# Order of the convolution kernel's set-up, and of the head's first transposes, in a state-space and gated-MLP kernel

## The chip, the cores and the metric

One core of a Trainium2 chip runs the program. The metric is the device time of one execution in microseconds (us); three timed runs of the kernel before are at hand, and one profiled execution.

## The reference, cut to what matters

`x` is 2 x 1024 rows of 512. Each row is normalised. From the normalised rows come a convolution along the row, whose 512 taps are made from 64 complex states (Lambda, p, q, B, Ct), and a gated MLP whose three weights carry low-rank additions (rank 16).

```
xn = _layernorm(x)
# convolution kernel K (512 taps), from the states
g = 2.0 / step * ((1.0 - Omega) / (1.0 + Omega))
denom = g[:, None] - Lambda[None, :]
cauchy = lambda v: (v[None, :] / denom).sum(-1)
k00, k01, k10, k11 = cauchy of Ct*B, Ct*p, q*B, q*p
at_roots = c * (k00 - k01 * (1.0 / (1.0 + k11)) * k10)
K = ifft(at_roots, L).real
s = causal convolution of xn with K, plus D * xn
h1 = xn @ (w1 + 2 B1 A1).T ; h3 = xn @ (w3 + 2 B3 A3).T
g = silu((silu(h1) * h3) @ (w2 + 2 B2 A2).T)
out = x + s * g
```

## The kernel before

**Tiling.** The 2048 rows are cut into four blocks of 512 (block 0, a loop over blocks 1 and 2, block 3). The 1376 hidden units are cut into 11 tiles, j = 0 to 10. For each j there are three places: "gate" (product with w1's tile into `h1`), "up" (w3's tile into `h3`) and "down" (w2's tile j-1 into the four banks `f`). Every float32 operand is split in a high and a low part of type fp32r, and a product is three matmuls (lines 939 to 941), each 128x128 by 128x512. Five engines run instruction streams of their own, each in the order in which the code is written, and they meet by semaphores.

**Folds, in block 0 only.** `fold(kind, j)` on TensorE multiplies the low-rank factors of weight `kind` (1, 3 or 2) and tile j into one of two PSUM banks `spare0`, `spare1`, used in turn. VectorE adds it to the loaded weight (`fold_add`, line 728), which also frees the bank; ScalarE casts the high part (`fold_hi`, line 592); VectorE subtracts to get the low part (`fold_lo`, line 743; three of them are done by GpSimd). TensorE waits for both before it uses the tile (`wait_split`). A fold thus takes a bank that the fold two before it must have left. Folds (3, j+2) stand at place "up" and (1, j+2) at "gate" of tile j, (2, j) at "down". `hidden_mul` (line 792) multiplies silu(h1) by h3, ScalarE casts its high part (line 632), `hidden_lo` (line 797) gives the low part. The cast of tile j waits until TensorE has finished `down(j-1)` (semaphore `g_used`).

**The convolution kernel, beside the folds.** ScalarE scales a row of sines and cosines (line 671, waits for the load `trig_sb`). GpSimd turns that into denominators and their squared magnitude `mag`; then come three `fold_lo` of its own, then 35 small operations that make the vectors `vmat` ("the vectors"), then the product `res` with `1/mag`. VectorE makes the reciprocal in two halves at the places in `RECIPROCAL_AT`. TensorE multiplies `res` by `vmat` at `KAPPA_AT` into a spare bank ("kappa", line 1056); ScalarE copies it out (line 675); GpSimd works out the coefficients, stores them and loads them back as a row on all partitions (`coef_row`). VectorE multiplies the four parts of `dft_sb` by that row (`K_PRODUCTS_AT`) and sums them (`K_SUMS_AT`). The sum goes by three DMAs to the Toeplitz tile `tz`, which the convolution at the end of block 0 needs.

**The head.** TensorE runs the folds (1,0) and (3,0), transposes the four row tiles (`turn_rows(r)`), and the folds (1,1) and (3,1) stand between them. Per row tile ScalarE normalises (`rows_norm`), then casts the transposed tile (`rows_hi`), and VectorE makes its low part (`rows_lo`). The first 256 columns of tile 0 start when row tiles 0 and 1 are split. Beside that the factors of all other folds are split in `spread_hl` (lines 701, 887); after its low part SyncE issues six DMAs that lay them out in `lora_stack`, and behind these in the same queue the weights of the next tiles and `trig_sb`. `spare` and the table `SPARE` deal the banks in the order of use, so a moved kappa changes the banks of the folds between its old place and its new one.

Of the kernel before, what the change touches and what calls it, by code (L numbers as in the profile page):

```python
# [25 lines left out]
ALU = mybir.AluOpType  # L26
ACT = mybir.ActivationFunctionType
AXIS = mybir.AxisListType
# [151 lines left out]
RECIPROCAL_AT = [(2, "down"), (3, "down")]  # L180

KAPPA_AT = (5, "gate")
K_PRODUCTS_AT, K_SUMS_AT = (7, "gate"), (7, "up")
# [3 lines left out]
K_PARTS = D // P  # L187
# [59 lines left out]
def build(nc, x, xT, w1, w3, w2, lora, lora_st, lora_mv, s4_lanes, s4_vc, s4_bp, s4_scalars, trig, lanes, dft, outT):  # L247
    ctx = ExitStack()
    with ctx:
# [337 lines left out]
        def _(act):  # L587
# [6 lines left out]
            def rows_hi(r):  # L594
                act.wait_ge(xt_turned, r + 1)
                nc.scalar.copy(xt[:, 0, 0, :, r * P:(r + 1) * P],
                               f[r][:, :].rearrange("p (c u) -> p c u", c=DC)).then_inc(xhi_done, 1)
# [101 lines left out]
            rows_hi(0)  # L699
            act.wait_ge(spread_in, 32)  # L700
            nc.scalar.copy(spread_hl[:, 0, :], spread[:, :]).then_inc(spread_hi, 1)
            rows_norm(2)
            rows_hi(1)
# [14 lines left out]
        def _(dve):  # L718
# [108 lines left out]
            def body(b, par, par_next, first, last):  # L827
# [4 lines left out]
                for j in range(HT):  # L832
                    for place in ("gate", "up", "down"):
# [11 lines left out]
                        if first and (j, place) == K_PRODUCTS_AT:  # L845
                            dve.wait_ge(dft_in, 16)
                            dve.wait_ge(coef_row_in, 16)
                            for h in range(K_PARTS):
                                nc.vector.tensor_tensor(dft_sb[:, h, :], dft_sb[:, h, :], coef_row[:, :], ALU.mult) \  # L849
                                    .then_inc(k_products, 1)  # L850
                        if first and (j, place) == K_SUMS_AT:
                            dve.wait_ge(k_products, K_PARTS)
                            nc.vector.tensor_reduce(kcol[:, :], dft_sb[:, :, :], AXIS.X, ALU.add).then_inc(k_summed, 1)
                        if place == "up":
                            hidden_lo(b, j)
                        if first and (j, place) in RECIPROCAL_AT:
                            n = RECIPROCAL_AT.index((j, place))
                            dve.wait_ge(mag_ready, 1)
                            part = mag[:, n * D // len(RECIPROCAL_AT):(n + 1) * D // len(RECIPROCAL_AT)]
                            nc.vector.reciprocal(part, part).then_inc(inv_ready, 1)  # L860
                        for c in () if last else norm_at.get((j, place), ()):
                            next_shift(b + 1, c, par_next)
# [20 lines left out]
            fold_add(3, 0)  # L883
            fold_lo(1, 0)
            rows_lo(0)
# [3 lines left out]
            rows_lo(1)  # L889
# [15 lines left out]
        def _(pe):  # L905
# [66 lines left out]
            def start():  # L972
# [9 lines left out]
                turn_rows(0)  # L982
                fold(1, 1)
                turn_rows(1)
                fold(3, 1)
# [4 lines left out]
                for c in range(DC):  # L990
                    pe.matmul(h1[:, lo], w13_tile(1, 0, 0)[:, c, :], xt[:, 0, 0, c, lo], start=(c == 0), stop=False)
                turn_rows(3)
# [132 lines left out]
        def _(pool):  # L1125
            steps = [0]

            def then(ins):

                steps[0] += 1  # L1130
                ins.then_inc(s4_step, 1)
                pool.wait_ge(s4_step, steps[0])
# [59 lines left out]
            pool.wait_ge(den_ready, 3)  # L1192
            then(tt(den_im[:, :], den_im[:, :], res[:, :], ALU.add))
            then(tt(mag[:, :], den_re[:, :], den_re[:, :], ALU.mult))
            then(tt(res[:, :], den_im[:, :], den_im[:, :], ALU.mult))
            tt(mag[:, :], mag[:, :], res[:, :], ALU.add).then_inc(mag_ready, 1)
            for kind, j in POOL_LO:
                fold_lo(kind, j)

# [22 lines left out]
            pool.wait_ge(v_ready, 1)  # L1222

# [56 lines left out]
            pool.wait_ge(k_summed, 1)  # L1280
# [74 lines left out]
```

## Time and profile before

| | |
|---|---|
| median of 3 runs | 411.18 us (411.14 to 411.35) |
| the profiled execution | 411.04 us, of which its span is 409.2 us |
| TensorE matmuls busy | 403.8 us (99% of the span) |
| VectorE | 169.0 us (41%) |
| ScalarE | 106.6 us (26%) |
| GpSimd | 70.7 us (17%) |
| granted TensorE clock | 1.00 in the mean |
| chain that ended last | PE 93%, DVE 4%, issue 1% |

TensorE's busy time fills the span, so the time is the length of its stream plus the waits in it. The other engines count by what they make TensorE wait for. VectorE's 41% is a mean: in block 0 it is busy for 6 to 9 us of every 10, later for 2 to 4.

### The profile page before, as it was taken

The page shows a single profiled execution, that of the slowest core. Times are in us where ns is not written, and L with a number is a line of the kernel's source. Part 1 is how long each engine was busy: PE and PEld are TensorE (multiplying, and loading weights), DVE is VectorE, ACT ScalarE, POOL GpSimd, SP SyncE. Part 2 cuts the span into 40 slices and gives each one's busy share as a digit, 9 for nine tenths or more (in the row PEclk, how much of TensorE's full clock was granted, in tenths as well). Part 3 has the DMA queues.
Part 4 walks back from the last instruction along what each step waited for, and adds up shares of the span by engine and source line. Part 5 has one row for each costly group of instructions (what it writes and reads, how often), then busy time and mean ns, then how long its engine had stood idle before and what let it go on. Part 6 is the DMA issues. An engine that isn't in the chain of part 4 may idle for free.

```text
span 409.2 us, 5001 instructions
## 1 busy us (share of the span) xinstructions
PE 403.8 (99%) x1850; PEld 336.9 (82%) x1850; DVE 169.0 (41%) x264; ACT 106.6 (26%) x174; POOL 70.7 (17%) x140
## 2 busy tenths in 40 slices
PE   8999999999999999999999999999999999999996
PEld 8988888878888888888888888888888888888885
DVE  5777776783792322142343222133334111211125
ACT  7654332222351111222221111112222111111122
POOL 6237737510800114000000102300000000000000
PEclk9999999999999999999999999999999999999999
DMA  7673933403425101000016101000002000000002
GB/s 267 175 274 114 318 110 89 98 9 96 154 77 181 51 2 52 2 0 0 0 48 202 61 0 52 0 0 0 0 0 103 2 0 0 2 0 0 2 0 103
DMA packets 14514, 27.02 MB, mean 66 GB/s; under 512 B 2672, under 2 KB 4720, under 8 KB 14368
## 3 DMA queue, kind: packets, MB, share of 16 engines
q1 hardware_dynamic: 13872, 25.40, 19.3%
q0 software_dynamic: 336, 0.86, 1.1%
q10 hardware_dynamic: 288, 0.52, 0.3%
q8 instruction: 11, 0.18, 0.2%
q14 instruction: 7, 0.06, 0.0%
HBM read 21.48 MB, written 4.54 MB: 64 GB/s over the span
## 4 chain that ended last, share of the span: by engine, by line
PE 93%; DVE 4%; issue 1%; ACT 0%; DVEq 0%; POOL 0%; ACTq 0%; POOLq 0%
PE h L939 19%; PE h L940 19%; PE h L941 19%; PE f L939 10%; PE f L940 10%; PE f L941 10%; PE h L962 2%; PE spare L926 2%; PE h L970 1%; DVE raw L728 1%; PE spare L941 1%; PE spare L940 1%; PE spare L939 1%; PE spare L921 1%; DVE dft_sb L849 1%
## 5 line engine op out<-in xcount | busy, mean ns | idle before, releaser
L939 PE MATMUL h<-xt,w 128*128 (+2 forms) x340 | 131.2, 386 | 0.0
L940 PE MATMUL h<-xt,w 128*128 (+2 forms) x340 | 131.1, 386 | 0.0
L941 PE MATMUL h<-xt,w 128*128 (+2 forms) x340 | 131.1, 386 | 0.0
L941 PEld LDWEIGHTS h<-xt,w 128*128 128x128 f32 x340 | 63.9, 188 | 12.9
L939 PEld LDWEIGHTS h<-xt,w 128*128 128x128 f32 x340 | 63.9, 188 | 12.7
L940 PEld LDWEIGHTS h<-xt,w 128*128 128x128 f32 x340 | 63.9, 188 | 12.5
L792 DVE TENSOR_TENSOR g<-g,h 128x512 f32<-128x512 f32 x40 | 27.5, 688 | 108.5 <-PE h L941 108.3
L939 PE MATMUL f<-ghl,w2f 128*128 128x512 f32 x176 | 68.7, 390 | 0.8 <-DVE w2f L743 0.8
L797 DVE TENSOR_TENSOR ghl<-g,ghl 128x512 fp32r<-128x512 f32 x44 | 31.6, 718 | 90.2 <-ACT ghl L632 90.2
L940 PE MATMUL f<-ghl,w2f 128*128 128x512 f32 x176 | 68.6, 390 | 0.0
L941 PE MATMUL f<-ghl,w2f 128*128 128x512 f32 x176 | 68.5, 389 | 0.0
L632 ACT CAST ghl<-g 128x512 fp32r<-128x512 f32 x44 | 27.3, 621 | 156.4 <-PE f L941 143.5
L939 PEld LDWEIGHTS f<-ghl,w2f 128*128 128x128 f32 x176 | 33.0, 188 | 7.7 <-DVE w2f L743 1.0
L941 PEld LDWEIGHTS f<-ghl,w2f 128*128 128x128 f32 x176 | 33.0, 188 | 6.9
L940 PEld LDWEIGHTS f<-ghl,w2f 128*128 128x128 f32 x176 | 33.1, 188 | 6.5
L615 ACT ACTIVATE g<-h 128x512 f32<-128x512 f32 x40 | 23.9, 598 | 45.3 <-PE h L941 45.1
L728 DVE SCALAR_TENSOR_TENSOR raw<-spare,raw 128x512 f32<-128x512 f32 (+2 forms) x33 | 22.3, 677 | 2.2 <-DVE raw L728 1.1
L1138 POOL TENSOR_TENSOR scales<-moments,lane_c 128x2 f32<-128x2 f32 x6 | 1.6, 258 | 119.5 <-DVE moments L755 119.5
L592 ACT CAST w<-raw 128x512 fp32r<-128x512 f32 (+1 forms) x22 | 13.4, 610 | 29.8 <-DVE raw L728 29.7
L1138 POOL TENSOR_TENSOR normal_rows<-xres,scale_rows 128x512 f32 (+1 forms) x12 | 16.0, 1365 | 13.5 <-DMA scale_rows<-scales_scratch 13.5
L743 DVE TENSOR_TENSOR w<-raw,w 128x512 fp32r<-128x512 f32 (+1 forms) x17 | 12.7, 751 | 0.4 <-DVE raw L728 0.2
L592 ACT CAST w2f<-raw 128x512 fp32r<-128x512 f32 (+1 forms) x11 | 6.8, 622 | 18.1 <-DVE raw L728 18.1
(133 smaller groups left out, 309.9 us busy)
## 6 DMA issues: line engine op xcount, KB each, us to landing
raw<-w_dram SPq DMA_DIRECT2D x28, 256.0 KB, 4.1
xres<-xT_dram SPq DMA_DIRECT2D x4, 1024.0 KB, 7.0
outT_dram<-xres SPq DMA_DIRECT2D x15, 256.0 KB, 2.4
rows_next<-x_dram SPq DMA_DIRECT2D x4, 512.0 KB, 3.8
scale_rows<-scales_scratch SPq DMA_DIRECT2D x3, 512.0 KB, 4.0
dft_sb<-dft_dram SPq DMA_DIRECT2D x1, 1024.0 KB, 9.3
rows<-x_dram SPq DMA_DIRECT2D x2, 512.0 KB, 6.8
raw<-w_dram SPq DMA_DIRECT2D x4, 224.0 KB, 2.5
```

Of the source, the lines that this page charges most:

```text
L592: nc.scalar.copy(folded(kind, j, 0), raw_tile(kind, j)).then_inc(whi_done, 1)
L615: nc.scalar.activation(g[:, :], h1[:, :], ACT.Silu).then_inc(silu_done, 1)
L632: nc.scalar.copy(ghl[:, 0, :], g[:, :]).then_inc(ghi_done, 1)
L728: nc.vector.scalar_tensor_tensor(out=rt, in0=low, scalar=LORA_SCALE, in1=rt, op0=ALU.mult, op1=ALU.add) \
L743: nc.vector.tensor_tensor(folded(kind, j, 1), raw_tile(kind, j), folded(kind, j, 0).bitcast(F32), ALU.subtract).then_inc(wlo_done, 1)
L792: nc.vector.tensor_tensor(g[:, :], g[:, :], h3[:, :], ALU.mult).then_inc(g_done, 1)
L797: nc.vector.tensor_tensor(ghl[:, 1, :], g[:, :], ghl[:, 0, :].bitcast(F32), ALU.subtract).then_inc(glo_done, 1)
L926: mm = pe.matmul(bankt[:, n * units:(n + 1) * units], fac[:, a + c * P:a + (c + 1) * P], fac[:, bc + t0 * P:bc + t0 * P + units], start=Tr ...
L939: pe.matmul(out, w[1], m[0], start=start, stop=False)
L940: pe.matmul(out, w[0], m[1], start=False, stop=False)
L941: return pe.matmul(out, w[0], m[0], start=False, stop=stop)
L1138: return nc.gpsimd.tensor_tensor(out, a, c, op)
```

## The change

Four edits. (1) In the head TensorE turns row tile 1 ahead of fold (1,1), and fold (3,1) goes behind the first four matmuls of tile 0; ScalarE normalises row tile 2 and casts row tile 1 ahead of the spread factors' high half; VectorE takes row tiles 0 and 1 ahead of fold (1,0)'s low half and of the spread factors' low half. (2) GpSimd makes the vectors ahead of the denominators. (3) The second reciprocal moves from (3, "down") to (3, "up"), kappa from (5, "gate") to (4, "up"). (4) The products move from (7, "gate") to two at (6, "up") and two at (7, "gate"), the sum from (7, "up") to one half at (7, "gate") and one at (7, "up"); products, sums and reciprocal now stand ahead of `hidden_lo` of the same place.

```diff
-RECIPROCAL_AT = [(2, "down"), (3, "down")]
-KAPPA_AT = (5, "gate")
-K_PRODUCTS_AT, K_SUMS_AT = (7, "gate"), (7, "up")
+RECIPROCAL_AT = [(2, "down"), (3, "up")]
+KAPPA_AT = (4, "up")
+K_PRODUCTS_AT = {(6, "up"): (0, 1), (7, "gate"): (2, 3)}
+K_SUMS_AT = {(7, "gate"): slice(0, 2), (7, "up"): slice(2, 4)}
...
             rows_hi(0)
+            rows_norm(2)
+            rows_hi(1)
             act.wait_ge(spread_in, 32)
             nc.scalar.copy(spread_hl[:, 0, :], spread[:, :]).then_inc(spread_hi, 1)
-            rows_norm(2)
-            rows_hi(1)
...
-                        if first and (j, place) == K_PRODUCTS_AT:
+                        if first and (j, place) in K_SUMS_AT:
+                            parts = K_SUMS_AT[j, place]
+                            dve.wait_ge(k_products, parts.stop)
+                            nc.vector.tensor_reduce(kcol[:, parts], dft_sb[:, parts, :], AXIS.X, ALU.add).then_inc(k_summed, 1)
+                        if first and (j, place) in K_PRODUCTS_AT:
                             dve.wait_ge(dft_in, 16)
                             dve.wait_ge(coef_row_in, 16)
-                            for h in range(K_PARTS):
+                            for h in K_PRODUCTS_AT[j, place]:
...
-                        if place == "up":
-                            hidden_lo(b, j)
                         if first and (j, place) in RECIPROCAL_AT:
...
+                        if place == "up":
+                            hidden_lo(b, j)
...
+            rows_lo(0)
             fold_lo(1, 0)
-            rows_lo(0)
+            rows_lo(1)
             dve.wait_ge(spread_hi, 1)
             nc.vector.tensor_tensor(spread_hl[:, 1, :], spread[:, :], spread_hl[:, 0, :].bitcast(F32), ALU.subtract) \
                 .then_inc(spread_lo, 1)
-            rows_lo(1)
...
                 turn_rows(0)
+                turn_rows(1)
                 fold(1, 1)
-                turn_rows(1)
-                fold(3, 1)
                 turn_rows(2)
...
                     pe.matmul(h1[:, lo], w13_tile(1, 0, 0)[:, c, :], xt[:, 0, 0, c, lo], start=(c == 0), stop=False)
+                fold(3, 1)
                 turn_rows(3)
...
             pool.sem_inc(small_ready, 1)
-            pool.wait_ge(den_ready, 3)
...
-            for kind, j in POOL_LO:
-                fold_lo(kind, j)
...
             pool.wait_ge(v_ready, 1)
 
+            pool.wait_ge(den_ready, 3)
+            then(tt(den_im[:, :], den_im[:, :], res[:, :], ALU.add))
...
+            for kind, j in POOL_LO:
+                fold_lo(kind, j)
+
             pool.wait_ge(inv_ready, len(RECIPROCAL_AT))
...
-            pool.wait_ge(k_summed, 1)
+            pool.wait_ge(k_summed, len(K_SUMS_AT))
```

VectorE at tile 7, before: fold_add (1,9), the four products, `hidden_mul`, fold_lo (1,9), fold_add (3,9), the sum, `hidden_lo`.

```order
L728 SCALAR_TENSOR_TENSOR raw_76<-spare0,raw_76 128x448 [waits fold_ready,raw_in1]
L849 TENSOR_TENSOR dft_sb_86<-dft_sb_86,coef_row_77 128x512 [waits fold_added,coef_row_in,dft_in]
L849 TENSOR_TENSOR dft_sb_86<-dft_sb_86,coef_row_77 128x512 x3
L792 TENSOR_TENSOR g_57<-g_57,h3 128x512 [waits h3_ready,silu_done]
L743 TENSOR_TENSOR w13_49<-raw_76,w13_49 128x2x224 [waits whi_done]
L728 SCALAR_TENSOR_TENSOR raw_76<-spare1,raw_76 128x448 [waits fold_ready,raw_in5]
L853 TENSOR_REDUCE kcol_74<-dft_sb_86 128x4 [waits fold_added,k_products]
L797 TENSOR_TENSOR ghl_52<-g_57,ghl_52 128x512 [waits ghi_done]
```

VectorE from tile 6 "up" on, now: fold_add (3,8), two products, `hidden_lo(6)`, fold_lo (3,8), fold_add (2,6), the moments of rows 2 and 3, fold_lo (2,6).

```order
L729 SCALAR_TENSOR_TENSOR raw_76<-spare0,raw_76 128x512 [waits fold_ready,raw_in4]
L854 TENSOR_TENSOR dft_sb_86<-dft_sb_86,coef_row_77 128x512 [waits fold_added,coef_row_in,dft_in]
L854 TENSOR_TENSOR dft_sb_86<-dft_sb_86,coef_row_77 128x512
L798 TENSOR_TENSOR ghl_52<-g_57,ghl_52 128x512 [waits ghi_done]
L744 TENSOR_TENSOR w13_49<-raw_76,w13_49 128x512 [waits whi_done]
L729 SCALAR_TENSOR_TENSOR raw_76<-spare1,raw_76 128x512 [waits fold_ready,raw_in2]
L753 BN_STATS stats_61<-rows_1_94 128x6 [waits fold_added,rows_in1]
L756 BN_AGGR moments_62<-stats_61 128x2 [waits stats_done]
L753 BN_STATS stats_61<-rows_1_94 128x6 [waits rows_in1]
L756 BN_AGGR moments_62<-stats_61 128x2 [waits stats_done]
L744 TENSOR_TENSOR w2f_50<-raw_76,w2f_50 128x512 [waits whi_done]
```

The wait for `coef_row_in` stood behind fold_add (1,9); now it stands ahead of `hidden_lo(6)` and of all that follows it.

ScalarE at tiles 4 and 5, before: the high cast of the hidden tile 4, then the casts and the silu of the next places, and the copy of kappa.

```order
L632 CAST ghl_52<-g_57 128x512 [waits g_used,g_done]
L592 CAST w2f_50<-raw_76 128x512 [waits fold_added]
L615 ACTIVATE g_57<-h1 128x512 [waits glo_done,h1_ready]
L592 CAST w13_49<-raw_76 128x512 [waits fold_added]
L675 COPY kap_71<-spare0 128x32 [waits kappa_ready]
```

ScalarE there, now:

```order
L633 CAST ghl_52<-g_57 128x512 [waits g_used,g_done]
L676 COPY kap_71<-spare0 128x32 [waits kappa_ready]
L593 CAST w2f_50<-raw_76 128x512 [waits kappa_copied,fold_added]
L616 ACTIVATE g_57<-h1 128x512 [waits glo_done,h1_ready]
```

The copy of kappa moved up past two casts and a silu, and stands right behind the cast that waits for `g_used`.

VectorE in the head, before, from fold_add (3,0) on: the low half of fold (1,0), of row tile 0 (`f0`), of the spread factors, of row tile 1 (`f1`), of fold (3,0).

```order
L728 SCALAR_TENSOR_TENSOR raw_76<-spare1,raw_76 128x512 [waits fold_ready,raw_in4]
L743 TENSOR_TENSOR w13_49<-raw_76,w13_49 128x512 [waits fold_added,whi_done]
L765 TENSOR_TENSOR xt_51<-f0,xt_51 128x4x128 [waits xhi_done]
L887 TENSOR_TENSOR lora_spread_split_80<-lora_spread_79,lora_spread_split_80 128x708 [waits spread_hi]
L765 TENSOR_TENSOR xt_51<-f1,xt_51 128x4x128 [waits xhi_done]
L743 TENSOR_TENSOR w13_49<-raw_76,w13_49 128x512 [waits whi_done]
```

VectorE in the head, now:

```order
L729 SCALAR_TENSOR_TENSOR raw_76<-spare1,raw_76 128x512 [waits fold_ready,raw_in4]
L766 TENSOR_TENSOR xt_51<-f0,xt_51 128x4x128 [waits fold_added,xhi_done]
L744 TENSOR_TENSOR w13_49<-raw_76,w13_49 128x512 [waits whi_done]
L766 TENSOR_TENSOR xt_51<-f1,xt_51 128x4x128 [waits xhi_done]
L890 TENSOR_TENSOR lora_spread_split_80<-lora_spread_79,lora_spread_split_80 128x708 [waits spread_hi]
L744 TENSOR_TENSOR w13_49<-raw_76,w13_49 128x512 [waits whi_done]
```

The spread factors' low half, which SyncE's six stack loads wait for, moved one row down; those of the row tiles moved up.

## Rows read from the trace of the kernel before

**Rows 1.** Waits of TensorE's weight loads; us in total, times, longest.
```profile
PEld f L939 <- DVE w2f L743: 1.0, 1, 1.0
```

**Rows 2.** Timeline, TensorE, hidden tiles 7 and 8: start, length, instruction, idle before.
```profile
80.12 0.41 PE L939 MATMUL f<-ghl,w2f 128*128 128x512 f32 x1
...
88.78 0.45 PE L926 MATMUL spare<-lora_stack 128*128 128x224 f32 x2
...
90.07 0.50 PE L939 MATMUL f<-ghl,w2f 128*128 128x512 f32 x1 [0.84 <-DVE w2f L743]
```

**Rows 3.** Timeline, VectorE, hidden tiles 6 to 8.
```profile
72.48 0.69 DVE L728 SCALAR_TENSOR_TENSOR raw<-spare,raw 128x512 f32<-128x512 f32 x1
...
74.89 0.69 DVE L797 TENSOR_TENSOR ghl<-g,ghl 128x512 fp32r<-128x512 f32 x1 [1.72 <-ACT ghl L632]
...
78.80 0.66 DVE L743 TENSOR_TENSOR w2f<-raw,w2f 128x512 fp32r<-128x512 f32 x1
...
80.22 2.50 DVE L849 TENSOR_TENSOR dft_sb<-dft_sb,coef_row 128x512 f32<-128x512 f32 x4 [0.23 <-DMA coef_row<-coef_scratch]
...
84.55 2.29 DVE L853 TENSOR_REDUCE kcol<-dft_sb 128x4 f32<-128x2048 f32 x1 [0.16 <-DVE raw L728]
...
89.32 0.69 DVE L743 TENSOR_TENSOR w2f<-raw,w2f 128x512 fp32r<-128x512 f32 x1 [0.69 <-ACT w2f L592]
```

**Rows 4.** Timeline, TensorE and ScalarE around the kappa product.
```profile
52.48 0.40 PE L939 MATMUL f<-ghl,w2f 128*128 128x512 f32 x1
...
55.00 0.39 PE L941 MATMUL f<-ghl,w2f 128*128 128x512 f32 x1
...
58.41 0.95 PE L1056 MATMUL spare<-vmat,res 128*128 128x8 f32 x8
...
60.57 0.62 ACT L592 CAST w<-raw 128x512 fp32r<-128x512 f32 x1 [1.23 <-DVE raw L728]
...
61.10 0.18 ACT L675 COPY kap<-spare 128x32 f32<-128x32 f32 x1
```

**Rows 5.** Timeline of GpSimd on the convolution kernel.
```profile
40.38 0.69 POOL L1135 TENSOR_SCALAR vtmp<-lane_d,lane_c 128x1 f32<-128x1 f32 x2
...
54.02 1.62 POOL L1138 TENSOR_TENSOR res<-den_im,mag 64x512 f32<-64x512 f32 x1
...
71.78 0.97 POOL L1268 DMA_DIRECT2D coef_scratch<-coef  x1 [0.31 <-POOL coef L1138]
```

**Rows 6.** Waits of GpSimd and ScalarE on the denominators; us in total, times, longest.
```profile
POOL den_im L1138 <- ACT res L671: 13.2, 1, 13.2
...
ACT den_re L671 <- DMA trig_sb<-trig_dram: 1.2, 1, 1.2
```

**Rows 7.** DMA issues: tensors, queue, count, KB, median us from issue to landing.
```profile
coef_scratch<-coef POOLq DMA_DIRECT2D x1, 2.0 KB, 4.1
...
k_row<-kcol POOLq DMA_DIRECT2D x1, 2.0 KB, 1.7
```

**Rows 8.** Timeline, VectorE, hidden tile 3: the low half and a reciprocal.
```profile
47.20 0.71 DVE L797 TENSOR_TENSOR ghl<-g,ghl 128x512 fp32r<-128x512 f32 x1 [1.73 <-ACT ghl L632]
...
49.25 1.75 DVE L860 RECIPROCAL mag<-mag 128x256 f32<-128x256 f32 x1
```

**Rows 9.** Timeline, VectorE, head: the spread factors' low half.
```profile
11.60 0.89 DVE L887 TENSOR_TENSOR lora_spread_split<-lora_spread,lora_spread_split 128x708 fp32r<-128x708 f32 x1
```

**Rows 10.** Timeline, SyncE: the last of six stack loads.
```profile
16.77 0.60 SPq L545 DMA_DIRECT2D lora_stack<-lora_spread_split  x1
```

**Rows 11.** DMA issues of that stretch: KB, us from issue to landing.
```profile
lora_stack<-lora_spread_split SPq DMA_DIRECT2D x1, 204.0 KB, 3.9
```

**Rows 12.** Timeline, TensorE: the first fold that needs the stack.
```profile
21.33 0.40 PE L921 MATMUL spare<-lora_stack 128*128 128x512 f32 x1
```

**Rows 13.** Timeline, VectorE and TensorE: folds of tiles 3 and 4.
```profile
33.40 0.68 DVE L728 SCALAR_TENSOR_TENSOR raw<-spare,raw 128x512 f32<-128x512 f32 x1
...
34.14 0.64 PE L926 MATMUL spare<-lora_stack 128*128 128x256 f32 x4
```

More of the change, by code:

```diff
@@ L844, in body @@
                             late = now[-1:]
-                        if first and (j, place) == K_PRODUCTS_AT:
+                        if first and (j, place) in K_SUMS_AT:
[3 more added lines that the diff above has]
+                        if first and (j, place) in K_PRODUCTS_AT:
                             dve.wait_ge(dft_in, 16)
                             dve.wait_ge(coef_row_in, 16)
-                            for h in range(K_PARTS):
+                            for h in K_PRODUCTS_AT[j, place]:
                                 nc.vector.tensor_tensor(dft_sb[:, h, :], dft_sb[:, h, :], coef_row[:, :], ALU.mult) \
                                     .then_inc(k_products, 1)
-                        if first and (j, place) == K_SUMS_AT:
-                            dve.wait_ge(k_products, K_PARTS)
-                            nc.vector.tensor_reduce(kcol[:, :], dft_sb[:, :, :], AXIS.X, ALU.add).then_inc(k_summed, 1)
-                        if place == "up":
-                            hidden_lo(b, j)
                         if first and (j, place) in RECIPROCAL_AT:
@@ L1191, in _ @@
             pool.sem_inc(small_ready, 1)
-            pool.wait_ge(den_ready, 3)
[L1193 to L1196, printed above, removed]
-            for kind, j in POOL_LO:
-                fold_lo(kind, j)
             then(ts(vtmp[:, 0:1], lane_d[:, 3:4], lane_c[:, SIGN:SIGN + 1], ALU.mult))
@@ L1222, in _ @@
             pool.wait_ge(v_ready, 1)
+            pool.wait_ge(den_ready, 3)
+            then(tt(den_im[:, :], den_im[:, :], res[:, :], ALU.add))
+            then(tt(mag[:, :], den_re[:, :], den_re[:, :], ALU.mult))
+            then(tt(res[:, :], den_im[:, :], den_im[:, :], ALU.mult))
+            tt(mag[:, :], mag[:, :], res[:, :], ALU.add).then_inc(mag_ready, 1)
+            for kind, j in POOL_LO:
+                fold_lo(kind, j)
             pool.wait_ge(inv_ready, len(RECIPROCAL_AT))
```

## The prediction, made before the change was timed

> **What bounds the kernel now.** I read the engines' busy times first: TensorE's matmuls fill the span at the full clock, so a change that leaves their number alone can only act through waits in TensorE's stream. The waits of its weight loads come next. Apart from the program's start and the head they have one entry: the load for a `down` product waits 1.0 us for VectorE's low half of a w2 tile [rows 1]. The timeline puts it at hidden tile 8. Fold (3,10) is issued at 88.78, two short matmuls of 0.23 us together, and `down(7)` follows at 90.07 instead of 89.0 [rows 2]. So 1.1 us are lost there, and no change to this stretch can return more. VectorE is why. It reaches the four products at 80.22, just when the coefficient row lands, spends 2.5 us on them and 2.3 us on the sum, and so finishes fold_lo (2,7) only at 90.0 [rows 3]. One tile earlier it is not late: fold_lo (2,6) ends at 79.46 and `down(6)` starts at 80.12, a margin of 0.7 us [rows 2, 3]. The time of the result is thus a race of VectorE's queue against two points, 80.1 and 89.0. A first race, in the head, is between the factors' way to the stack and TensorE.
>
> **Vectors ahead of denominators.** GpSimd idles 13.2 us ahead of the denominators [rows 6]; the vectors run from 40.38 until the product `res` follows at about 52.6, 12.2 us [rows 5]. Moved into the idle time they cost nothing, with 1 us to spare; if they ran longer the denominators would start later by the excess, which the idle time behind GpSimd's last fold_lo absorbs. `res` then waits only for the second reciprocal. That one takes 1.75 us and moves into a wait of 1.73 us that VectorE has ahead of `hidden_lo(3)` [rows 8], so it is free, and it ends near 47.4. Two products on GpSimd, some 3 us, bring `res` to 50.4, where it was at 55.6 [rows 5].
>
> **Kappa at (4, "up").** TensorE comes there at 52.48, ahead of `down(3)` [rows 4]. `res` is 2 us earlier than that, so TensorE does not wait; the product itself takes 0.8 us of its stream at either place. But ScalarE's copy stands behind the cast of hidden tile 4, and that cast waits for `g_used`, the end of `down(3)`. `down(3)` ends at 55.4 now, and at 56.2 with kappa ahead of it; with 0.1 for the semaphore and 0.5 from the start of a cast to that of the copy behind it (60.57 to 61.10), the copy comes at 56.8 [rows 4]. That is 4.3 us earlier than 61.10, where TensorE's product is 5.9 earlier. GpSimd's arithmetic from the copy to the store at 71.78 and the two DMAs behind it take what they took, since nothing of it was changed [rows 4, 5]. The row lands at 80.2 - 4.3 = 75.9.
>
> **Products and sums.** VectorE is through with fold_add (3,8) at 73.3 [rows 3] and now waits for the row until 75.9. Before, only `hidden_lo(6)` waited there, until 74.89. Behind the new wait are queued two products, `hidden_lo(6)`, fold_lo (3,8), fold_add (2,6), two moments and fold_lo (2,6). In sum: two products are 1.2 us; from `hidden_lo(6)` to the end of fold_lo (2,6) it is 4.6 us [rows 3]. So fold_lo (2,6) ends at 75.9 + 5.8 = 81.7, and `down(6)`, which wants 80.12, starts at 81.8: **a new wait of 1.7 us.** Onwards: 1.4 us to the place of the products, half a sum 1.15, two products 1.2, 1.8 to the second half, another 1.15, and 3.2 to the end of fold_lo (2,7) [rows 3]. From the start of that fold_lo (2,6), 81.05, this gives 91.0. TensorE, 1.7 us late, could start `down(7)` at 90.7 and waits 0.3 more. `down(7)` starts at 91.05, where it started at 90.07: **+1.0 us**. The split is not to blame for it; the work is the same 4.8 us. The place is: 4.3 us of earlier start buy less than the 5.2 us of other work that now stands behind the first products. The bounds of this term: -1.1, where the row comes early enough for both waits to go, and +1.8, if the row comes 0.8 us later, by operations of GpSimd that are slowed beside VectorE's.
>
> **Head.** Row tile 1's low half stood behind the spread factors' (0.8 us from that one's start to the next [rows 9]); TensorE's first products wait for it. Its own work (a transpose, four matmuls, fold (3,1)) and fold (3,0)'s low half, which comes no earlier, leave an estimated 0.5 us of this at most, 0 at least. The price: the spread factors' low half starts 0.6 us later, one operation of its queue, and with it every DMA of SyncE behind it. The last stack load is issued at 16.77 and lands 3.9 us later, at 20.7 [rows 10, 11]; the fold that needs it is at 21.33, its weights loaded at 21.1 [rows 12]. Now the load lands at 21.3, and TensorE is there at 20.9. The gain is gone: the fold starts at 21.4. Behind the stack in the same queue is `trig_sb`, for which ScalarE already waits 1.2 us [rows 6]. ScalarE's casts, GpSimd's denominators and VectorE's low halves follow it 0.6 us late, up to fold_add (1,4), which ends at 34.08. TensorE's fold (3,4), which needs that bank, is the second half of the row at 34.14, its load near 34.25 [rows 13]. A margin of 0.1 us against a delay of 0.6 makes **+0.5 us**. Between the ends -0.5 (neither the stack nor the sines hold it up) and +0.6 I take the upper part, because each link of this chain is back to back in the trace.
>
> **The sum.** The profiled execution took 411.04 us; +1.0 and +0.5 make 412.5. The median is 0.14 above it: **412.7 us**. No later wait on TensorE exists in which either could hide, and the sum of the kernel is ready for `tz` still several us before it is needed, so 1 us more there is free.
>
> **Rivals.** (a) *One of the two waits does not come.* The delay in the head is absorbed, or the row lands 1 us earlier: 411.2 to 411.9. For it: both margins are a few tenths. Against it: no slack is visible in either chain. (b) *Faster.* The coefficient store takes 4.1 us, but the store of the sum, of the same 2 KB on the same queue, takes 1.7 [rows 7]. If the first, at another moment of the weights' traffic, did the same, the row would land at 73.5, fold_lo (2,6) at 79.3 and fold_lo (2,7) at 88.6, both in time: -1.1, and with the head between -0.5 and +0.5, 409.6 to 410.6. Against it: the coefficients go out in pieces of 8 bytes, the sum in pieces of 16, and weights are loaded in the new window as in the old. (c) *Slower than the forecast, kappa holds TensorE.* GpSimd's `res` must be there at 52.48, 2 us after my estimate; from there on every us of lateness costs TensorE one, and all that follows too. One us beyond gives 413.7. It would take the reciprocal 3 us later, for which nothing in the rows speaks. (d) *Kappa is of no use:* if the copy on ScalarE came out later still, the row would land at 76.9 and the time were 413.7.
>
> The Trainium skill, "DMA: Bandwidth & Descriptors", section "Anatomy of one DMA — SWDGE (gpsimd) path", gives a DMA of GpSimd's queue a fixed part of about 2.0 us and says that it is nearly constant. By it the store would land 2.1 us earlier than by the 4.1 of its row, and rival (b) would be the forecast; the trace agrees for the sum's store (1.7) and disagrees for the very transfer that is at stake.
>
> **How the numbers follow.** Forecast (412.0 to 413.3): 0.55. Rival (a) 0.22, rival (b) 0.13, rivals (c) and (d) 0.10. Three runs tell 0.2% from no change, 0.8 us here. Slower by over that (above 412.0): 0.55 and 0.10, less some of the forecast's lower edge, 0.60. Within it: (a), that edge and the upper part of (b): 0.28. Faster: 0.12. The range leaves out the better half of (b) and the worst of (c): 410.6 to 413.6.
>
> **What would show it.** In the profile after: a wait of VectorE on the coefficient row, 2 to 3 us, ahead of the first product; a wait of TensorE on the low half of w2 at `down(6)`, near 80, of 1.7 us, and a short one at `down(7)`; the copy of kappa right behind a cast at 56.8 to 57.4; the first fold from `lora_stack` at about 21.4 with a wait ahead of it; a wait of half a us near 34.3. I am wrong if the row lands before 74.5, or if the fold at 34 runs without a wait.

## The result

The changed kernel takes 413.67 us (median of 6 runs, 412.96 to 414.21), the kernel before 411.22 us beside it (6 runs, 410.78 to 411.99): ratio 1.0060, 95% interval 1.0049 to 1.0071. It is 2.4 to 2.5 us slower. The prediction said slower, 412.7 us, with 413.6 as its upper end; the direction holds, the size does not, and the range misses the time by 0.07 us.

The profiled execution took 414.13 us with a span of 412.3 us; that of before had 411.04 and 409.2. So 3.1 us have to be found in the span. In the rows of after the line numbers are one to two higher than in those of before; experiments that add lines shift them by up to six more.

### The profile page after: what moved, and what is told of

Its sections match the earlier page's. It is cut to its first block, busy times and chain, and to the rows that moved or that the text cites. A ratio compares the mean times of both kernels' runs of the same rounds, so it can differ in the third digit from the quotient of the medians.

```text
span 412.3 us, 5004 instructions
## 1 busy us (share of the span) xinstructions
PE 403.8 (98%) x1850; PEld 336.3 (82%) x1850; DVE 170.2 (41%) x265; ACT 106.4 (26%) x174; POOL 70.0 (17%) x140
## 4 chain that ended last, share of the span: by engine, by line
PE 84%; DVE 5%; DMA 3%; POOL 3%; issue 2%; SPq 1%; ACT 0%; DVEq 0%; POOLq 0%; ACTq 0%
PE h L943 17%; PE h L941 17%; PE h L942 17%; PE f L941 9%; PE f L943 9%; PE f L942 9%; POOL cplx L1140 2%; PE h L964 2%; DMA lora_stack<-lora_spread_split 1%; DMA xn<-x_dram 1%; DMA coef_row<-coef_scratch 1%; SPq L546 1%; DVE raw L729 1%; PE spare L928 1%; PE spare L943 1%
```

## The profile after, read against the one before

The page first, row of TensorE in its part on busy times. 403.8 us are what it was before, so the 3.1 us are waits.

```profile
PE 403.8 (98%) x1850; PEld 336.3 (82%) x1850; DVE 170.2 (41%) x265; ACT 106.4 (26%) x174; POOL 70.0 (17%) x140
```

The waits of the stretch from 76 to 95 us (engine, result, line, releaser: us in total, times, longest), which answer to [rows 1], where one entry of 1.0 us stood:

```profile
DVE dft_sb L854 <- DMA coef_row<-coef_scratch: 3.9, 1, 3.9
...
PEld h L941 <- DVE w L744: 2.5, 1, 2.5
...
PEld f L941 <- DVE w2f L744: 0.6, 2, 0.4
```

VectorE waits 3.9 us for the coefficient row, and TensorE's largest wait is not for a w2 tile (`w2f`, a `down` product) but for a tile of w3 (`w`, result `h`): an `up` product. TensorE's timeline, start and length, shows where. It answers to [rows 2, 12, 13].

```profile
22.04 0.47 PE L923 MATMUL spare<-lora_stack 128*128 128x512 f32 x1 [1.05 <-DMA lora_stack<-lora_spread_split]
...
34.94 0.86 PE L928 MATMUL spare<-lora_stack 128*128 128x256 f32 x4
...
77.97 0.38 PE L928 MATMUL spare<-lora_stack 128*128 128x224 f32 x2
...
80.67 0.47 PE L941 MATMUL h<-xt,w 128*128 128x512 f32 x1 [2.32 <-DVE w L744]
```
```profile
83.89 0.50 PE L941 MATMUL f<-ghl,w2f 128*128 128x512 f32 x1
```
```profile
92.67 0.38 PE L928 MATMUL spare<-lora_stack 128*128 128x224 f32 x2
93.23 0.50 PE L941 MATMUL f<-ghl,w2f 128*128 128x512 f32 x1 [0.18 <-DVE w2f L744]
```

The first fold from the stack, at 21.33 before, starts at 22.04. The fold at 34.14 starts at 34.94, behind the shift. At 77.97 stands the fold that precedes `up(7)`; two short matmuls of it take 0.2 us together, so `up(7)` was due at 78.2 and starts at 80.67, **2.5 us late**. `down(6)` (83.89) loses 0.2 us more, `down(7)` (93.23) 0.3. `down(7)` stood at 90.07, so it is 3.16 us later than before, and with that the whole difference of the spans has been made by hidden tile 8.

VectorE in the same stretch answers to [rows 3]:

```profile
73.52 0.68 DVE L729 SCALAR_TENSOR_TENSOR raw<-spare,raw 128x512 f32<-128x512 f32 x1
78.07 1.29 DVE L854 TENSOR_TENSOR dft_sb<-dft_sb,coef_row 128x512 f32<-128x512 f32 x2 [3.86 <-DMA coef_row<-coef_scratch]
79.28 0.69 DVE L798 TENSOR_TENSOR ghl<-g,ghl 128x512 fp32r<-128x512 f32 x1
79.88 0.68 DVE L744 TENSOR_TENSOR w<-raw,w 128x512 fp32r<-128x512 f32 x1
...
83.18 0.66 DVE L744 TENSOR_TENSOR w2f<-raw,w2f 128x512 fp32r<-128x512 f32 x1
```

It is through with fold_add (3,8) at 74.2 and stands still until the row lands. Behind the two products follow `hidden_lo(6)` and, at 79.88, fold_lo (3,8), whose end at 80.56 releases TensorE at 80.67.

ScalarE and GpSimd, to be read beside [rows 4, 5]:

```profile
57.40 0.62 ACT L633 CAST ghl<-g 128x512 fp32r<-128x512 f32 x1 [1.31 <-PE f L943]
57.93 0.18 ACT L676 COPY kap<-spare 128x32 f32<-128x32 f32 x1
```
```profile
58.25 1.17 POOL L1140 TENSOR_TENSOR cplx<-kap 128x4 f32<-128x4 f32 x2 [6.46 <-ACT kap L676]
...
69.61 0.97 POOL L1270 DMA_DIRECT2D coef_scratch<-coef  x1 [0.31 <-POOL coef L1140]
...
74.20 0.57 POOL L1275 DMA_DIRECT2D coef_row<-coef_scratch  x1 [2.56 <-DMA coef_scratch<-coef]
```

The copy of kappa stands behind the cast that waits for `down(3)`, and comes at 57.93. From the copy to the store of the coefficients are now 11.68 us, where they were 10.68 (61.10 to 71.78).

## Experiments

Ratios are to the kernel before, timed on the same chip beside each (411.16 us beside `set_lows` and `spaced_spread_first`, 411.32 beside the others). "C" is the moment at which the first product on the coefficient row starts.

### One part of the change alone

`head_only` is the kernel before with edit 1, the head. `conv_only` is the changed kernel with the head of before, so it has edits 2 to 4. For example, on TensorE in `conv_only`:

```diff
                 turn_rows(0)
-                turn_rows(1)
                 fold(1, 1)
+                turn_rows(1)
+                fold(3, 1)
                 turn_rows(2)
...
-                fold(3, 1)
                 turn_rows(3)
```

> The kernel before with the head of the change alone (edit 1). Theory H, the stack of factors comes late: the first fold from lora_stack waits 0.5 to 1.2 us, and fold (3,4) near 34 is late too; the time is +0.5 to +1.0 us above before, 411.7 to 412.2. Rival H0, the head gives back its half us and the whole loss is in the convolution kernel's part: -0.5 to 0 us, 410.7 to 411.2, and no wait at that fold.

Measured: 410.91 us (410.69 to 412.12, 11 runs), ratio 0.9993 (0.9984 to 1.0002). No loss by the median, as rival H0 has it, though not without a wait: its profiled execution, the slowest of the eleven (412.12), shows two small waits in the head. TensorE there:

```profile
21.16 0.47 PE L921 MATMUL spare<-lora_stack 128*128 128x512 f32 x1 [0.21 <-DMA lora_stack<-lora_spread_split]
...
34.66 0.51 PE L926 MATMUL spare<-lora_stack 128*128 128x256 f32 x2 [0.19 <-DVEq L732]
```

Behind them the first `down` product stands at 35.01, 0.4 us later than before. The rest of this execution's 1.1 us comes later, where VectorE waits 0.73 us for the coefficient row at tile 7 (0.23 in [rows 3]).

> The changed kernel with the head of before (edits 2 to 4 alone). Theory C, the coefficient row is late for products that stand ahead of fold_lo (3,8): VectorE waits 3 to 4 us for the row at tile 6, TensorE waits some 1.5 to 2.5 us at up(7), and the time is +1.0 to +2.1 us, 412.2 to 413.3. Rival: the head carries the loss through its delay of ScalarE and GpSimd, and this kernel is within 0.3 us of before.

Measured: 414.57 us (413.37 to 414.60, 5 runs), ratio 1.0078 (1.0065 to 1.0090). That is above the range of theory C, whose waits are there. So the slowdown comes from edits 2 to 4, and all of it: with the head added to them the median is 0.9 us lower (414.57 to 413.67; 0.7 by the ratios, whose intervals just overlap). The profiled execution of `conv_only` is its fastest, 413.37. VectorE and TensorE:

```profile
77.28 1.29 DVE L854 TENSOR_TENSOR dft_sb<-dft_sb,coef_row 128x512 f32<-128x512 f32 x2 [4.11 <-DMA coef_row<-coef_scratch]
```
```profile
79.88 0.47 PE L941 MATMUL h<-xt,w 128*128 128x512 f32 x1 [2.56 <-DVE w L744]
...
92.45 0.50 PE L941 MATMUL f<-ghl,w2f 128*128 128x512 f32 x1 [0.21 <-DVE w2f L744]
```

`down(7)` at 92.45 is 2.38 us behind [rows 2], as the two executions' times are (413.37 against 411.04). VectorE starts the first product at C = 77.28 after a wait of 4.11 us. From C to `down(7)` are 15.17 us, in the changed kernel 15.16. In these two kernels VectorE's queue behind the first product is thus a rigid chain, and the end of the stretch moves with C.

### Kappa copied earlier

The copy was queued behind the cast that waits for `down(3)`. `copy_first` is the changed kernel with the copy ahead of the casts of that place; `conv_copy_first` has the head of before besides.

```diff
                             hidden(b, j)
+                        if first and (j, place) == KAPPA_AT:
+                            act.wait_ge(kappa_ready, 1)
+                            nc.scalar.copy(kap[:, :, :], ...).then_inc(kappa_copied, 1)
+                            act.wait_ge(kappa_copied, 1)
+                            act.sem_inc(spare_free[...], 1)
                         if first:
                             for kind, t in folds(place, j):
                                 fold_hi(kind, t)
...
-                        if first and (j, place) == KAPPA_AT:
-                            (the same five lines, behind the casts)
```

> The changed kernel, with ScalarE's copy of kappa at the start of place (4, up), ahead of the cast that waits for down(3). Theory C with the cast as the cause of the late row: the copy comes 3.4 us earlier (54.5 instead of 57.9), the row lands near 74.6, VectorE waits at most 0.5 us for it, TensorE waits neither at up(7) nor at down(7); what is left is the head's +0.5 to +1.0 less the 1.1 us that before lost at down(7): 410.6 to 411.2. Rival R, VectorE's work at tile 6 (two products more ahead of the low halves) is what costs, whenever the row lands: TensorE still waits over 1 us at up(7) or down(6), 412.3 or more.

Measured: 410.43 us (409.75 to 411.66, 7 runs), ratio 0.9984 (0.9970 to 0.9998). The copy is at 54.39, 3.5 us earlier than in the changed kernel, and the time falls by 3.2 us, slightly below theory C's range. ScalarE and VectorE:

```profile
54.39 0.19 ACT L662 COPY kap<-spare 128x32 f32<-128x32 f32 x1 [0.63 <-PE spare L1058]
```
```profile
74.32 1.29 DVE L854 TENSOR_TENSOR dft_sb<-dft_sb,coef_row 128x512 f32<-128x512 f32 x2 [0.23 <-DVE raw L729]
```

It no longer waits for the row, and TensorE has no wait in hidden tiles 6 to 8. The place of one 0.2 us copy in ScalarE's queue is all that this run changes. So with the products at (6, "up") that place, and the row that depends on it, makes the slowdown.

> The same early copy with the head of before. Theories C and H together: nothing of the change's loss is left and the wait of 1.1 us at down(7) is gone, 410.1 (409.9 to 410.4), under both kernels. Rival R: 411.5 or more. Rival H0: no better than copy_first.

Measured: 410.67 us (410.00 to 411.05, 12 runs), ratio 0.9984 (0.9976 to 0.9993). The copy is at 53.41, the store is issued at 64.64. The median misses the expected 409.9 to 410.4. In this profile the store takes 5.5 us, the longest of all profiles, and VectorE still waits 1.6 us:

```profile
coef_scratch<-coef POOLq DMA_DIRECT2D x1, 2.0 KB, 5.5
```
```profile
74.72 1.29 DVE L854 TENSOR_TENSOR dft_sb<-dft_sb,coef_row 128x512 f32<-128x512 f32 x2 [1.59 <-DMA coef_row<-coef_scratch]
```
```profile
89.88 0.50 PE L941 MATMUL f<-ghl,w2f 128*128 128x512 f32 x1 [0.20 <-DVE w2f L744]
```

C + 15.16 = 89.88: the chain holds here too, to the last digit. `down(7)` gains only 0.2 us over before in this execution.

### Other places for the products

Both have the head of before, and the copy where the change has it. `products_7` puts all four products and the whole sum back to tile 7 and keeps the rest of the change:

```diff
-K_PRODUCTS_AT = {(6, "up"): (0, 1), (7, "gate"): (2, 3)}
-K_SUMS_AT = {(7, "gate"): slice(0, 2), (7, "up"): slice(2, 4)}
+K_PRODUCTS_AT = {(7, "gate"): (0, 1, 2, 3)}
+K_SUMS_AT = {(7, "up"): slice(0, 4)}
```

`products_down` moves the first two one place on:

```diff
-K_PRODUCTS_AT = {(6, "up"): (0, 1), (7, "gate"): (2, 3)}
+K_PRODUCTS_AT = {(6, "down"): (0, 1), (7, "gate"): (2, 3)}
```

> The changed kernel with the head of before, all four products back at (7, gate) and the sum whole at (7, up): vectors first, the reciprocal at (3, up) and kappa at (4, up) stay. Theory C, the place of the first products is what costs: the row lands at 77 to 78.5, VectorE comes for it at 80.2 and does not wait, TensorE waits 1.1 us at down(7) as before; 411.0 to 411.5, no difference from before. Rival: the earlier kappa, the reciprocal ahead of the low half or the vectors beside the head cost something themselves; 411.8 or more.

Measured: 411.22 us (410.72 to 411.73, 11 runs), ratio 0.9997 (0.9988 to 1.0006). TensorE:

```profile
90.32 0.50 PE L941 MATMUL f<-ghl,w2f 128*128 128x512 f32 x1 [0.84 <-DVE w2f L744]
```

The wait of before is back in its old size [rows 2], 0.84 us. The vectors, the reciprocal and kappa at their new places cost nothing that can be measured. The row's load is issued at 73.63 and lands 4.1 us later, at 77.7; VectorE starts the products at 80.48. With a row that is there 2.7 us early they gain nothing either: 2.5 us of products and 2.3 us of sum in one tile are what holds `down(7)`.

> The changed kernel with the head of before, and the first two products one place later, at (6, down), behind hidden_lo(6), fold_lo (3,8) and fold_add (2,6). Theory C: TensorE no longer waits at up(7); with the row at 77.3 the rest of VectorE's queue ends at 90.3 where it ended at 90.0, so +0.3 us, and up to +1.5 where the row lands later: 411.5 to 412.7, with a wait of about 1 us at down(6). Rival, the wait is set by the row alone and the place within tile 6 does not matter: +2.4 to +3.2 us as with the head of before, 413.6 or more.

Measured: 411.43 us (410.93 to 412.19, 11 runs), ratio 1.0006 (0.9997 to 1.0015). VectorE waits 0.4 us for the row. TensorE:

```profile
81.27 0.50 PE L941 MATMUL f<-ghl,w2f 128*128 128x512 f32 x1 [0.70 <-DVE w2f L744]
...
90.61 0.50 PE L941 MATMUL f<-ghl,w2f 128*128 128x512 f32 x1 [0.21 <-DVE w2f L744]
```

At `down(7)` the product is 0.5 us later than before, and the waits are split over two tiles; the time is that of before within the noise. One place makes 3.1 us of median (414.57 to 411.43): at (6, "up") the row is 4 us away, at (6, "down") 0.4.

### Why GpSimd takes 1.0 us longer

The groups of GpSimd's work on the coefficients (count, busy us, mean ns of one), in the kernel before:

```profile
L1138 POOL TENSOR_TENSOR cplx<-kap 128x4 f32<-128x4 f32 x4 | 0.8, 206 | 6.0 <-ACT kap L675 5.8
```

and in `conv_only`:

```profile
L1140 POOL TENSOR_TENSOR cplx<-kap 128x4 f32<-128x4 f32 x4 | 1.5, 374 | 6.8 <-ACT kap L676 6.6
```

The same four operations on 4 columns take nearly twice as long, all of it in the first two, 1.17 us for 0.49. In time they stand right beside two subtractions of VectorE. GpSimd and VectorE in `conv_only`:

```profile
57.22 1.17 POOL L1140 TENSOR_TENSOR cplx<-kap 128x4 f32<-128x4 f32 x2 [6.56 <-ACT kap L676]
```
```profile
57.03 0.69 DVE L798 TENSOR_TENSOR ghl<-g,ghl 128x512 fp32r<-128x512 f32 x1 [2.65 <-ACT ghl L633]
57.64 0.69 DVE L744 TENSOR_TENSOR w<-raw,w 128x512 fp32r<-128x512 f32 x1
```

`hidden_lo(4)` waits for the cast of hidden tile 4, and the copy of kappa, for which GpSimd waits, stands right behind that cast. So the two engines start within 0.2 us of each other (57.03 and 57.22). `set_lows` replaces just these two subtractions by writes of zeros:

```diff
+                if isinstance(b, int) and t == 4:
+                    nc.vector.memset(ghl[:, 1, :].bitcast(F32), 0.0).then_inc(glo_done, 1)
+                    return
                 nc.vector.tensor_tensor(ghl[:, 1, :], g[:, :], ghl[:, 0, :].bitcast(F32), ALU.subtract)...
...
+                if (kind, j) == (3, 6):
+                    nc.vector.memset(folded(kind, j, 1).bitcast(F32), 0.0).then_inc(wlo_done, 1)
+                    return
                 nc.vector.tensor_tensor(folded(kind, j, 1), ..., ALU.subtract)...
```

> The convolution's part of the change with the head of before, and two of VectorE's low halves right behind the kappa copy, the hidden values' of tile 4 and weight (3,6)'s, set to zero by a memset instead of subtracted. These two low parts are left out of the matmuls' values; every instruction that waits or is waited for stays. Theory A (GpSimd's small operations stand still while VectorE runs an operation with two inputs from SBUF): GpSimd's first two products on kappa take 0.49 us together as in before, not 1.17, and the time from the end of kappa's copy to the coefficients' store falls from 11.68 us to 11.0 (10.8 to 11.2). Theory B (the first products are slow because they stand first behind a long wait, or because kappa has just been written): the pair stays at 1.1 to 1.2 us and the way to the store at 11.7. The end moves by no more than that 0.7 us in either case: TensorE's wait at up(7) 1.8 to 2.0 us by A, 2.4 to 2.6 by B, with the store's own landing (3.5 to 5.5 us in the profiles so far) read apart.

(The expectation says "from the end of kappa's copy"; its 11.68 us are counted from the copy's start, as everywhere here.) Measured in one profiled execution, 412.8 us. GpSimd, VectorE and TensorE:

```profile
57.10 0.49 POOL L1146 TENSOR_TENSOR cplx<-kap 128x4 f32<-128x4 f32 x2 [6.45 <-ACT kap L676]
```
```profile
57.04 0.48 DVE L802 MEMSET ghl<- 128x512 f32 x1 [2.76 <-ACT ghl L633]
57.59 0.48 DVE L745 MEMSET w<- 128x512 f32 x1
```
```profile
79.32 0.47 PE L947 MATMUL h<-xt,w 128*128 128x512 f32 x1 [2.12 <-DVE w L747]
...
91.88 0.50 PE L947 MATMUL f<-ghl,w2f 128*128 128x512 f32 x1 [0.21 <-DVE w2f L747]
```

The pair takes 0.49 us again instead of 1.17, with a write still beside it. It still stands first behind a long wait and still reads a fresh kappa, so neither of these slowed it. The copy is at 56.78 and the store at 67.91, 11.13 us, 0.55 less: 0.68 us are saved in the pair, and 0.13 are given back on balance by later operations, which now meet other subtractions. That is theory A. TensorE's wait at `up(7)` is 2.1 us, 0.1 above A's range.

`down(7)` comes 0.57 us earlier than in `conv_only`, and the span is 411.0 us against 411.6. That equals GpSimd's 0.55 us, but in part by chance: between these two executions the copy came 0.12 us earlier, the way from the store to the row's issue was 0.24 us shorter, and the row took 0.35 us longer.

The rest of the 1.0 us was not tested by itself, but the other profiles show what it is: a balance of which operations meet a subtraction. The two that multiply kappa by intermediate values took 0.47 us in before; in `conv_only` they take 1.24 us from 66.06 on, while VectorE runs `hidden_lo` at 65.96 and a fold_lo at 66.57. Before had its own slow ones, such as a pair with 0.86 us at 63.12, beside a fold_lo at 62.95, that has 0.48 in `conv_only`. In `spaced` (below), where the copy comes first, the pair takes 0.49 us although it too stands first behind a wait; it runs beside a fold_add (53.66), which reads one input from SBUF and one from PSUM. Three operations of intermediate values, 0.76 us in before and in `conv_only`, meet the subtractions at 56.96 and 57.57 there:

```profile
53.73 0.49 POOL L1140 TENSOR_TENSOR cplx<-kap 128x4 f32<-128x4 f32 x2 [3.03 <-ACT kap L662]
...
56.87 1.45 POOL L1140 TENSOR_TENSOR cplx<-cplx 128x4 f32<-128x4 f32 x3
```

From the copy to the store are 10.6 to 10.7 us in the two profiles with the old place of kappa, 11.2 to 11.3 in the five with the copy first, and 11.7 in the four with the copy behind the cast and the subtractions kept.

The Trainium skill, "SBUF — State Buffer", section "Who interferes with whom", says that a VectorE instruction with two inputs from SBUF contends with a GpSimd instruction that reads SBUF, and one with at most one such input, outside the modes that use both of VectorE's ports, does not. The trace agrees: 1.17 us beside subtractions, 0.49 beside writes and 0.49 beside a fold_add.

### The work spread over the tiles

If C must be early and VectorE's 4.8 us must not stand in one tile, the copy goes first, three products go to (6, "down"), where the row has been there for some us (issued at 70.02, 3.6 us to landing, first product at 76.93), and two of the moments, which nobody wants soon, leave that place.

```diff
-MOMENTS_AT_FIRST = {(4, "down"): (0,), (5, "down"): (1,), (6, "down"): (2, 3)}
+MOMENTS_AT_FIRST = {(4, "down"): (0, 1), (5, "down"): (2, 3)}
-K_PRODUCTS_AT = {(6, "up"): (0, 1), (7, "gate"): (2, 3)}
+K_PRODUCTS_AT = {(6, "down"): (0, 1, 2), (7, "gate"): (3,)}
```

`spaced` has this, the copy first and the head of before; `spaced_head` the same with the head of the change.

> Head of before, ScalarE's copy of kappa first at (4, up), products at (6, down) for three parts and at (7, gate) for one, and the moments of the next block a place earlier (two at (4, down), two at (5, down)). The row lands before 76.5 even if the coefficient store takes 5.5 us, and the queue of VectorE at tile 6 carries no more than before. Theory C: TensorE waits nowhere in tiles 6 to 8, 410.1 (409.9 to 410.3). Rival, VectorE is full in these tiles in any order: no better than 410.7.

Measured: 410.14 us (409.67 to 410.38, 7 runs), ratio 0.9971 (0.9960 to 0.9982). VectorE and TensorE in its profile (409.71 us, span 407.9):

```profile
76.93 1.90 DVE L854 TENSOR_TENSOR dft_sb<-dft_sb,coef_row 128x512 f32<-128x512 f32 x3 [0.21 <-DVE raw L729]
78.74 0.69 DVE L744 TENSOR_TENSOR w2f<-raw,w2f 128x512 fp32r<-128x512 f32 x1
...
87.45 0.69 DVE L744 TENSOR_TENSOR w2f<-raw,w2f 128x512 fp32r<-128x512 f32 x1 [0.69 <-ACT w2f L593]
```
```profile
88.93 0.41 PE L941 MATMUL f<-ghl,w2f 128*128 128x512 f32 x1
```

fold_lo (2,7) ends at 88.1, and `down(7)` follows its fold at 88.93 without a wait, 1.14 us earlier than in [rows 2]. That is the 1.1 us that the kernel before loses there, got back.

> The same with the head of the change. Theory H (the stack of factors comes late, the gain in the head is lost and more): 410.1 to 411.1, with a wait of 0.4 to 1.2 us at the first fold from lora_stack. Rival H0, the head gives what it was worth, 0.3 to 0.5 us: 409.6 to 409.8.

Measured: 409.89 us (409.44 to 411.33, 8 runs), ratio 0.9968 (0.9957 to 0.9978). The lowest median of all, but its distance to `spaced` is smaller than either spread, and it lies between the ranges of H and H0: it does not decide between them. The wait at the first fold is 0.2 us.

### The stack load in the head

`spaced_spread_first` is `spaced_head` with the spread factors' low half one row up on VectorE:

```diff
             rows_lo(0)
             fold_lo(1, 0)
-            rows_lo(1)
             (the spread factors' low half)
+            rows_lo(1)
             fold_lo(3, 0)
```

> The spaced version with the change's head (kappa copied first at (4,up), three products at (6,down), the moments at (4,down) and (5,down)), and on VectorE the spread factors' low half ahead of rows_lo(1) instead of behind it; TensorE and ScalarE keep the head's new order. Theory A (the head's price is the last stack load, which lands 21.1 to 22.2 where the spread's low half ends 0.7 us later, against 20.7 before): the stack's first fold stands at 20.7 to 21.1 without a wait on the DMA, the second row tile's low half comes 0.7 us later and TensorE waits some 0.3 to 0.6 us at turn_rows(1), so that the head gains nothing and the time is that of the spaced version with the head of before, ratio 0.997 (0.9955 to 0.9985) to the kernel before. Theory B (the load's landing varies by 1 us whatever its issue): a wait on the stack load stays possible, and the ratio is 0.9965, as with the change's head. Both inside 0.2% of each other in time; the row that tells them apart is the fold's start and what ended its wait.

Measured: 410.04 us (409.65 to 410.33, 7 runs), ratio 0.9971 (0.9960 to 0.9982), the same as both others. TensorE:

```profile
13.03 0.35 PE L998 MATMUL h<-xt,w 128*128 128x256 f32 x1 [0.41 <-DVE xt L766]
...
21.12 0.40 PE L923 MATMUL spare<-lora_stack 128*128 128x512 f32 x1
...
34.53 0.50 PE L928 MATMUL spare<-lora_stack 128*128 128x256 f32 x2 [0.21 <-DVEq L733]
```

The wait on the stack is gone, as theory A has it. Its other wait is there too, 0.41 us on row tile 1's low half, not at `turn_rows(1)` but at the first product that reads it: at 13.03, where `spaced_head` has it at 12.38 without a wait. Both ways bring TensorE to the fold from the stack at the same time, 21.12 and 21.07, against 21.27 in `spaced`. In the changed kernel, in `copy_first` and in `set_lows` the last stack load took 5.0, 5.2 and 5.3 us from issue to landing, in the nine other profiles 3.4 to 3.9. Its row of the changed kernel, beside [rows 11]:

```profile
lora_stack<-lora_spread_split SPq DMA_DIRECT2D x1, 204.0 KB, 5.0
```

The wait ahead of the first fold is 1.05 and 1.01 us in the first two, and 0.2 in `head_only` and `spaced_head`. That fits B as well: the duration changes from one kernel to the next without a change of the code at that place, and `set_lows`, with the head of before, had a long one and no wait. The second wait, near 34.6, stays. It is not the new head's alone: `products_7` and `products_down`, with the head of before, have the same delay. The four matmuls of that fold take 1.03 and 0.93 us there (0.64 in [rows 13]), and the first `down` product stands at 34.88 and 34.92.

## Why the prediction missed, point by point

**What bounds the kernel** held: TensorE's busy time did not change, and every us of difference is a wait of TensorE up to hidden tile 8. The kernel before loses 1.1 us at `down(7)`, and `spaced` shows that they can be had.

**Vectors, reciprocal, kappa's place free** held. In the profile of after GpSimd waits 0.61 us at 27.21 for the denominators, so the vectors fit into its idle time. `products_7`, with all three at their new places, is 0.9997.

**The copy of kappa.** Predicted 56.8 behind the cast; measured 56.90 in `conv_only` and, with the head's 1.03 us, 57.93 in the changed kernel. Held.

**"GpSimd's arithmetic from the copy to the store at 71.78 and the two DMAs behind it take what they took, since nothing of it was changed": the step that failed.** It gave C = 75.9. `conv_only` has 77.28: 0.1 from the copy, 1.0 from GpSimd's arithmetic (11.68 for 10.68 us), and 0.5 from the way of the store (4.94 us between the issues of the store and of the row's load, 4.43 before, with landings of 4.7 and 4.1 us), less 0.25 from the issue of the row's load to C (3.76 for 4.01). Why the store took longer is open. The instructions were the same, but the moment was new. The copy now ends beside `hidden_lo(4)`, and the first products meet two subtractions of VectorE. The prediction had this as the bound of its term, "operations of GpSimd that are slowed beside VectorE's", with 0.8 us; it was the likely case, since the cast releases VectorE and the copy right behind it releases GpSimd. With 77.28 in place of 75.9 the prediction's own sum gives 91.05 + 1.4 = 92.4 for `down(7)`. Measured: 92.45. So the chain behind the row was right, and the row was mis-sized.

**Size of the convolution's term.** Predicted +1.0, bounds -1.1 to +1.8. The profiled execution of `conv_only` has +2.4. Its median has +3.2, and this last 0.9 us stays open: the four other runs of that kernel are 0.8 to 1.2 us slower than the profiled one, and no profile shows them. The store, which took 3.5 to 5.5 us in the profiles, could be it, because the chain hands its time on one for one; this was not shown.

**Which wait.** The prediction put the wait at `down(6)`, 1.7 us. It stands at `up(7)`, whose fold_lo (3,8) is queued behind the same products. I listed this operation behind the new wait, but asked only for `down(6)` when TensorE wants what is queued. `up(7)` started at 77.2 before (its fold is at 76.94) and is the first demand. For the end it makes no difference, since TensorE arrives at `down(7)` behind VectorE in either case; for the reading of a profile it does.

**The head.** Predicted +0.5. The gain that it was made for is there: the first product with w3's tile 0 stands at 13.65 in the changed kernel and at 14.26 before. The profile of after seems to bear it out and more: the fold from the stack with 1.05 us of wait, and the first `down` product behind the fold near 34 at 35.64, 1.03 later than before. The runs say otherwise. Of four pairs that differ by the head alone, all have the lower median with the new head: 0.41 (`head_only`), 0.90 (after against `conv_only`), 0.24 (`copy_first`) and 0.25 us (`spaced_head`). The first is inside its interval, the others come from intervals that overlap. So the head costs nothing that can be measured. The two waits of the mechanism are there (both in `head_only` and in `spaced_head`), the second in two kernels with the old head as well, but the term was sized from a chain in which a delay of 0.6 us was passed on without loss. In the profiled executions the first `down` product behind the fold near 34 is at 34.87 to 35.01 with the new head, at 35.53 and 35.64 where the last stack load took 5 us, and at 34.48 to 34.92 with the old. Why the medians are better than these profiles was not found. One thing goes with the head in the profiles and was not tested: the coefficient store took 3.5 to 4.3 us in the five with the new head and 4.1 to 5.5 us in the seven with the old, and in the changed kernel C is only 0.79 us later than in `conv_only`, though its copy is 1.03 us later.

**The sum.** +1.0 and +0.5 were forecast; by medians it is +3.25 and -0.9. The two errors went opposite ways, so the total looks closer than its terms are; that is luck.

**Rivals.** (b), the faster store, is excluded for this transfer: 3.5 to 5.5 us in twelve profiles, never 1.7. The Trainium skill's fixed part of about 2.0 us ("DMA: Bandwidth & Descriptors", section "Anatomy of one DMA — SWDGE (gpsimd) path") does not describe it; the measurement decides. (c) did not come, TensorE did not wait for kappa. (d), the row later than thought, is what happened, by GpSimd and the store and not by ScalarE. It had 0.10 together with (c), and its row at 76.9 was still too early; that its 413.7 us is the measured median is the same luck as in the sum.

## What to carry to other kernels

When an operation is moved earlier, ask what the other engines run at the new moment: a pair of GpSimd's small operations took 1.17 us for 0.49 beside VectorE's two-input ones, and two releases that come from neighbouring instructions of one engine, here the cast and the copy, make the meeting certain. When a wait goes into an in-order queue, list everything queued behind it with the time at which each is first wanted, in the consumer's order, and take the row of a variable DMA at its slow end. An earlier result is worth nothing until the work that uses it has a place with room: here the early row needed the copy ahead of a blocked cast and VectorE's 4.8 us spread over two tiles (0.9971), while the earlier copy alone gave 0.9984 and later products alone 0.9997 and 1.0006.

## What the runs showed of the hardware that I had not expected

- A 2 KB store of GpSimd's queue, sent in pieces of 8 bytes, took 3.5 us in `copy_first` and 5.5 us in `conv_copy_first`, which differ by the head and by 1 us in when it is issued. The store of the sum, 2 KB in pieces of 16 bytes on the same queue, took 1.7 us in every profile.
- A pair of GpSimd operations on 4 columns took 1.17 us beside VectorE's subtractions of 512 columns (0.69 us each) and 0.49 us beside writes of 512 columns (0.48 us each) or beside an addition with one input from PSUM (0.69 us).
- The last of six stack loads, 204 KB, took 3.4 to 5.3 us over kernels with the same code at that place.
